# A convolution as products with diagonal matrices on the tensor engine, and the two batch elements of a quantiser taken one after the other

## The reference

```python
def bit_linear(x, w): return einsum('bsd,hd->bsh', act_quant(x), weight_quant(w))
def act_quant(x):                       # for each token
    scale = 127 / clip(max(abs(x), axis=-1), 1e-5)
    return clip(round(x * scale), -128, 127) / scale
# first block, hidden width 1024
h = bit_linear(x, w1)
h = depthwise_conv1d(h, conv_w, conv_b) # 3 taps along the tokens, padding 1
h = silu(h)
return bit_linear(h, w2)
# second block
return bit_linear(silu(bit_linear(x, w_gate)) * bit_linear(x, w_up), w_down)
```

## Time and profile before

| | us |
|---|---|
| median of 3 runs (lowest, highest) | 2870.0 (2860.18, 2885.66) |
| the profiled execution | 2874.32, span 2872.5 |
| busy: PE, DVE, ACT, POOL | 2015.8, 2128.5, 1306.5, 1243.8 |
| granted TensorE clock, mean share of full speed | 0.84 |

### The profile page before, as it was taken

One profiled execution on the slowest core, in us unless ns is written; L12 is line 12 of the kernel. 1 busy time (PEld: TensorE's weight loads), 2 busy tenths in 40 slices (PEclk: granted clock), 3 DMA queues, 4 the chain that ended last, 5 costly groups with the idle time before them and its releaser, 6 DMA issues.

```text
span 2872.5 us, 22420 instructions
## 1 busy us (share of the span) xinstructions
PE 2015.8 (70%) x7684; PEld 1072.3 (37%) x7684; DVE 2128.5 (74%) x2457; ACT 1306.5 (45%) x1838; POOL 1243.8 (43%) x535
## 2 busy tenths in 40 slices
PE   3786486677597847677668774777767966667775
PEld 1125362226322625223532253422452234542243
DVE  7753868995684495998768367799686827689967
ACT  1363445553155335654306443665421645356532
POOL 1030238991213024997211311599521221079942
PEclk9798588998789868899879976799977987689997
DMA  5500000000330000000061000000006100000000
GB/s 172 90 18 0 1 1 0 0 1 0 80 77 7 0 0 0 0 0 1 0 118 45 1 1 0 1 0 0 0 1 118 46 1 1 0 0 0 0 0 15
DMA packets 55914, 57.45 MB, mean 20 GB/s; under 512 B 8624, under 2 KB 50352, under 8 KB 55792
## 3 DMA queue, kind: packets, MB, share of 16 engines
q1 hardware_dynamic: 48880, 49.62, 6.8%
q10 hardware_dynamic: 6912, 6.29, 1.9%
HBM read 38.71 MB, written 16.79 MB: 19 GB/s over the span
## 4 chain that ended last, share of the span: by engine, by line
PE 44%; DVE 25%; POOL 14%; issue 7%; ACT 5%; DMA 3%; SPq 1%; ACTq 0%; POOLq 0%; DVEq 0%
PE psum L571 15%; PE psum L776 10%; POOL big L1507 9%; PE psum L671 4%; POOL big L1496 4%; DVE mid L1110 3%; PE psum L648 3%; PE psum L659 3%; PE psum L609 3%; DVE mid L1324 2%; PE psum L681 2%; ACT mid L833 2%; DVE big L1275 2%; DMA mid<-scratch 2%; DVE big L1149 2%
## 5 line engine op out<-in xcount | busy, mean ns | idle before, releaser
L776 PE MATMUL psum<-big,ident 128*128 128x512 f32 x992 | 524.0, 677 | 202.7 <-POOL big L1507 202.1
L1390 DVE TENSOR_TENSOR_SCAN big<-psum,b,big 128x512 f32<-128x512 f32 x512 | 613.9, 1259 | 0.0
L833 ACT ACTIVATE big<-psum 128x1024 f32<-128x1024 f32 (+2 forms) x592 | 451.9, 776 | 324.2 <-PE psum L659 252.1
L1507 POOL TENSOR_TENSOR big<-big 128x2048 f32<-128x2048 f32 x124 | 560.7, 4522 | 22.3 <-DVE big L1390 22.3
L833 ACT ACTIVATE psum<-mid,aneg 128x512 f32<-128x512 f32 x512 | 353.9, 692 | 265.0 <-DVE big L1390 265.0
L776 PEld LDWEIGHTS psum<-big,ident 128*128 128x128 f32 x992 | 202.1, 214 | 483.1 <-POOL big L1507 264.6
L1201 DVE TENSOR_REDUCE negmax<-psum 128x1 f32<-128x512 f32 x512 | 317.0, 678 | 68.1 <-PE psum L648 67.8
L648 PE MATMUL psum<-mid 96*128 96x512 bf16 x512 | 221.5, 438 | 65.6 <-DMA mid<-scratch 51.0
L1458 POOL TENSOR_TENSOR lsum<-lsum,onorm 128x512 f32<-128x512 f32 x32 | 40.6, 1270 | 523.7 <-ACT onorm L833 523.7
L1496 POOL TENSOR_TENSOR big<-mid,big 128x512 f32<-128x512 f32 (+1 forms) x128 | 222.9, 1742 | 20.0 <-ACT big L833 20.0
L1472 POOL TENSOR_TENSOR big<-big,mid 128x513 f32<-128x513 f32 x40 | 55.0, 1387 | 348.4 <-ACT big L833 348.4
(11 more groups left out here) (165 smaller groups left out, 3393.1 us busy)
## 6 DMA issues: line engine op xcount, KB each, us to landing
mid<-scratch SPq DMA_DIRECT2D x192, 64.0 KB, 2.2
scratch<-mid SPq DMA_DIRECT2D x4, 1536.0 KB, 6.0
mid<-scratch SPq DMA_DIRECT2D x48, 128.0 KB, 11.7
mid<-scratch ACTq DMA_DIRECT2D x48, 128.0 KB, 13.7
scratch<-big SPq DMA_DIRECT2D x4, 1536.0 KB, 25.8
out<-hres SPq DMA_DIRECT2D x8, 513.0 KB, 7.7
big<-in_x SPq DMA_DIRECT2D x8, 512.0 KB, 4.1
big<-in_w SPq DMA_DIRECT2D x2, 1024.0 KB, 6.3
```

Of the source, the lines that this page charges most:

```text
L776: mm = nc.tensor.matmul(y_psum[:, c], ident[:, :], st(1, k)[:, c], start=(n == 0), stop=(n == NS - 1))
L833: return nc.scalar.activation(o, a, func, **kw)
L1390: V.tensor_tensor_scan(st(0, k)[:, c], a_psum(DT * k + c), st(0, k)[:, c], b0[:, p, n, c:c + 1], ALU.mult, ALU.add).then_inc(scanned, 1)
L1507: G.tensor_tensor(st(1, k), st(0, k), c_row(k).unsqueeze(1).broadcast_to([P, DT, S]), ALU.mult).then_inc(hc_ready, 1)
```

## The change

In the first block, tiles 1, 2, 4 and 7 (`PE_CONV`) no longer get bias, middle tap and the two outer taps from ACT and DVE. PE computes all three taps: POOL prepares twelve 128 x 128 matrices, the identity with each row scaled by a tap (`tap(c, k)`, kept in `onorm`, which is free after attention), and PE multiplies the tile by them with the tile shifted by one column for each tap, in float32, into a PSUM slot of its own (`v{c}c`). ACT reads that slot, adds the bias and applies SiLU in one instruction. So that the shifted reads are defined at the edges, tiles of set 0 now lie 514 columns apart with a zero column ahead of each.

In both blocks the quantiser's second half is taken batch by batch: the transposes and rows of batch 0 come before those of batch 1 on PE, `scales(1, 0)` stands ahead of `absmax(1, 1)`, and DVE's multiplications and roundings alternate with `scales(1, 1)`. `absmax` of batch 0 stands one loop step earlier in both blocks.

```diff
+PE_CONV = (1, 2, 4, 7)
+CONV_LAG = 3
...
-    each(*[f"f{c}" for c in range(HT)])
+    for s in range(PAIR * HT + CONV_LAG):
+        if s < PAIR * HT:
+            order.append((f"f{s % HT}", s // HT))
+        if s >= CONV_LAG and (s - CONV_LAG) % HT in PE_CONV:
+            order.append((f"v{(s - CONV_LAG) % HT}c", (s - CONV_LAG) // HT))
...
         def big8(p, n):
-            o = p * 2 * W8 + n * W8
-            return big[:, o:o + W8].rearrange("p (c t) -> p c t", c=HT)
+            o = p * 2 * W8 + n * (W8 + 1)
+            if n:
+                return big[:, o:o + HT * T].rearrange("p (c t) -> p c t", c=HT)
+            return big[:, o:o + HT * (T + 1)].rearrange("p (c t) -> p c t", c=HT)[:, :, 1:T + 1]
...
+                def convolve(p, c):
+                    slot_free(f"v{c}c", p)
+                    o, f = slot(f"v{c}c", p), padded(p, c)
+                    for a, b in ((0, SPLIT), (SPLIT, T)):
+                        for k in range(3):
+                            mm = nc.tensor.matmul(o[:, a:b], tap(c, k), f[:, a + k:b + k], start=(k == 0), stop=(k == 2))
...
-                token_maxima(1)
-                token_rows(1)
+                for p in range(PAIR):
+                    token_maxima(1, (p,))
+                    token_rows(1, (p,))
...
-                    if 0 <= p < PAIR:
+                    if 0 <= p < PAIR and c not in PE_CONV:
                         act.wait_ge(f_pool if c in POOL_F else f_dve, tile_count(POOL_F, p, c))
...
+                    if 0 <= p < PAIR and c in PE_CONV:
+                        wait_full(act, f"v{c}c", p)
+                        run(big8(p, 1)[:, c], slot(f"v{c}c", p), ACT.Silu, bias=col("cb", c)).then_inc(f_silu, 1)
...
-                    if s == HT + 6:
+                    if s == HT + 5:
                         dve.wait_ge(f_silu, HT)
                         absmax(1, 0, big8(0, 1))
+                scales(1, 0)
                 dve.wait_ge(f_silu, HT * PAIR)
                 absmax(1, 1, big8(1, 1))
-                for p in range(PAIR):
-                    scales(1, p)
-                for p in range(PAIR):
-                    quantise(1, p, big8(p, 1), big8(p, 0), mid_bf(p, 5, HT), HT)
+                scale_tiles(1, 0)
+                scales(1, 1)
+                round_tiles(1, 0)
+                scale_tiles(1, 1)
+                round_tiles(1, 1)
...
-                    if s == HT + 4:
+                    if s == HT + 3:
                         dve.wait_ge(prod, HT)
                         absmax(3, 0, big8(0, 1))
+                scales(3, 0)
...
+                pool.wait_ge(unit_full, UNITS["O", PAIR - 1, 1] + 1)
+                for c in PE_CONV:
+                    for k in range(3):
+                        G.tensor_scalar(tap(c, k), ident[:, :], col("cw", 3 * c + k), 0.0, ALU.mult, ALU.add).then_inc(
+                            taps_ready, 1)
```

More of the change, by code:

```diff
@@ L94, in quantiser @@
     def quantiser(q):
-        each(f"T{q}")
-        each(f"I{q}", f"S{q}")
+        if q % 2:
+            each(f"T{q}", f"I{q}", f"S{q}")
+        else:
+            each(f"T{q}")
+            each(f"I{q}", f"S{q}")
     for p in range(PAIR):
@@ L112, in plan_fills @@
     each(*[f"z{c}" for c in range(DT)])
+    while len(order) % 4 != 2:
+        order.append(None)
     each("w0", "w1")
@@ L401, in build @@
         prod = signal("prod")
+        taps_ready = signal("taps_ready")
         raw_n = KT * HID
@@ L590, in layer_norm, with token_maxima @@
                         fill(f"var{q}", p, [(mean_w[:, :], sq[:, k]) for k in range(KT)])
-                def token_maxima(q):
-                    for p in range(PAIR):
+                def token_maxima(q, pairs=range(PAIR)):
+                    for p in pairs:
                         pe.wait_ge(absmax_part, q_of(q, p))
@@ L721, in _ @@
                 token_rows(0)
-                for p in range(PAIR):
-                    pe.wait_ge(q_ready, q_of(0, p))
-                    for c in range(HT):
-                        fill(f"f{c}", p, [(w1[:, k, c * P:(c + 1) * P], mid_bf(p, 1, 2)[:, k]) for k in range(KT)])
-                token_maxima(1)
-                token_rows(1)
+                for s in range(PAIR * HT + CONV_LAG):
+                    p, c = divmod(s, HT)
+                    if p < PAIR:
+                        if c == 0:
+                            pe.wait_ge(q_ready, q_of(0, p))
+                        fill(f"f{c}", p, [(w1[:, k, c * P:(c + 1) * P], mid_bf(p, 1, 2)[:, k]) for k in range(KT)])
+                    p, c = divmod(s - CONV_LAG, HT)
+                    if p >= 0 and c in PE_CONV:
+                        if s == CONV_LAG + PE_CONV[0]:
+                            pe.wait_ge(taps_ready, 3 * len(PE_CONV) + 2 * PAIR)
+                        pe.wait_ge(f_pool, tile_count(POOL_F, p, c))
+                        convolve(p, c)
+                for p in range(PAIR):
+                    token_maxima(1, (p,))
+                    token_rows(1, (p,))
                 for p in range(PAIR):
@@ L1467, in _ @@
                     G.memset(mid2(p, 3)[:, :, 0:1], 0.0).then_inc(pads, 1)
+                pool.wait_ge(unit_full, UNITS["O", PAIR - 1, 1] + 1)
[3 more added lines that the diff above has]
+                            taps_ready, 1)
+                for p in range(PAIR):
+                    for columns in pad_columns(p):
+                        G.memset(columns, 0.0).then_inc(taps_ready, 1)
                 for p in range(PAIR):
```

77 lines of the change are left out of this document (49 added, 28 removed).

## The result

| | before | after |
|---|---|---|
| median of 9 runs, us (lowest to highest) | 2871.2 (2860.18 to 2885.66) | 2851.8 (2838.79 to 2853.05) |
| the profiled execution, us | 2874.32 | 2838.79 |
| ratio after : before, 95% interval | | 0.992 (0.9899 to 0.9941) |

The change gains 0.8%.

A forecast was written before the change was run, and what follows sets the result against it. No engine was full; DVE alone was taken to bound the first block's tiles. (5.0 + 2.3 - 0.6) x 4 turns took 27 us off 2874.3, giving 2847; that execution lay 4.3 above the median, so 2843, range 2820 to 2866.

The forecast's parts named there:

- The taps: First block's tiles: tap work moved from DVE and ACT to PE brings X from 1050.0 to 1045.0, 5.0 us a turn.
- X: The end of the first block's second reduction over eight tiles, 1050.0 in the second turn before the change.
- C: Rival: PE at the low clock during the first block's convolutions, 12 us a turn slower, 2918 us; chance 0.12.
- The quantiser: First block from X to the last add: the new order takes 24.0 us against 26.3, 2.3 us gained a turn.
- The rounding: Quantiser's roundings on DVE: reading five runs and writing one takes 4.45 us a batch, the slow end, against 2.37.
- B: Rival: the rounding keeps its fast rate, 2.4 us for 4.45; 44 us off a run, 2826 us; chance 0.22.
- The second block: Second block: the second reduction begins later, behind slot reads and scales waiting for transposes; 0.6 us lost a turn.
- The sum: Whole run: 5.0 + 2.3 - 0.6 us a turn over 4 turns, 27 us off.
- D: Rival: hand-overs through PE, ACT and DVE eat the taps' gain, leaving 7 us a run, 2863 us; chance 0.21.

The follow-up runs named there:

- e6: The changed kernel with the first block's first reduction one step earlier in DVE's loop; ratio to before 0.9875.
- e11: The changed kernel with the quantisers' scaled tiles written without gaps, unscaled tiles still padded; 2829.1 us, ratio to before 0.9836.
- e3: The changed kernel with the rounded tiles also written with a gap between them and read so by PE; ratio to before 0.9873.
- e4: The kernel before with only the padded layout, set 0 in runs 514 columns apart; ratio to before 1.0053.
- e1: The kernel before with only the quantiser's new order, reductions at their old steps, table load moved; 2839.0 us, ratio to before 0.9886.
- e12: e11 and e6 together, with the second block's reduction of batch 0 back at its old step; 2819.4 us, ratio to before 0.9801.
- e8: The changed kernel with each convolution on PE cut to its middle product (wrong in value); one execution, 2842.4 us.
- e2: The changed kernel with both quantisers in the order of before and both reductions at their old steps; ratio to before 1.0007.

## Why the prediction was right, point by point

**The taps (5.0 us up to X).** Measured in the second turn: 3.9 (46.5 to 42.6). The bound moved to PE at the full clock, as said: granted clock 1.00 from 993 to 1025, and the last convolution ends at 1021.9, which settles C. A convolution took 2.76 where 2.6 was worked out from the float32 fills. The first reduction came at +22.4, predicted +22.0. The other two terms that were off are small: the second reduction started 12.9 behind the first, not 12.5, and took 7.29, not 7.0, with POOL's multiplication beneath it. The working named the left tap of tile 3 as what the first reduction stands behind, and DVE did wait 3.04 us there. It did not ask whether it has to stand there: e6 shows this place in the order to be worth 3 us a turn.

**The quantiser (2.3 us).** Measured 3.0: X to the end 23.3, predicted 24.0. Each station is within 0.3 us: batch 0 rounded at X + 8.7 (8.8), batch 1 at X + 17.6 (17.7). The working had POOL hold DVE's multiplication to X + 13.3; it took 4.43 and ended at X + 13.1. The end was 0.7 early because PE's second product ran at the full clock (1.00), 3.69 for the 4.4 that half of 8.83 gave.

**The rounding (4.45 a batch).** 4.49, with 2.83 for the five tiles. This was the open cost, and the end chosen was right; B is out for this kernel, and its price was near: 44 us a run was worked out for a fast rounding, and e11, which makes it fast, gains 48 by the blocks. Of the two reasons given one fails. The prediction took the slow end because the multiplication, too, has an operand that is not one run; but in e3 both operands of the rounding are in five runs, and it takes 2.90. What e3, e4 and e11 bear out is the comparison of source and destination: 2.37 for one run to one, 2.90 for five runs to five, 4.49 for five to one. The rule of the Trainium skill ("VectorE: DVE Perf Modes", section "What auto-detection actually checks") names outermost counts that are both even or equal; the trace agrees in all three cases.

**The second block (-0.6 us).** Measured -0.76 in the mean, -0.85 in the second turn, but by another split. Predicted was a second reduction 3.6 us late, because of the moved step with its slot reads, and the wait of `scales(3, 0)` for the transposes. It came 2.5 late, and e1 has nearly the same (+29.8) with the step unmoved: so the wait and the `scales` themselves are the cause. The step is worth 0.7 a turn (e12 against e11). The rest, from the last rounding to the last add, took 7.2 us for the 6.3 predicted, with PE's product at 5.26 and a granted clock of 0.69 in it, where 4.4 was reckoned.

**The sum.** 27 us predicted, 26.6 by the blocks, 35.5 between the two profiled executions, 19.4 between medians. That 27 and 26.6 agree is partly luck: in the second turn the taps gave 1.1 less than predicted and the quantiser 0.7 more, 24.3 us in four turns, and the rest comes from before's first and fourth turns, whose first blocks ended 1 us later. D (hand-overs eat the gain) is out as a whole, since the first reduction did move, but e8 shows where it begins: 3.4 us below the present pace.

**What the prediction did not see** is the sign of the parts. It gave 5.0 of 6.7 us to the products. Taken alone they and their layout give 1.1 us a turn (e2), and the order alone 7.5 (e1), because there it keeps the fast rounding: the slow one costs 5.4 us a turn with the new order (e11) and only 2.3 with the old (e4). The surplus of 5.75 and 5.13 in the earlier trace rows was named and priced, but inside the change, where slow rounding gives half of it back. Pricing each part against before on its own, from the same rows, would have shown a part that does better alone.

## What to carry to other kernels

Where a new layout serves one reader (here the shifted reads of a convolution), give the later consumers the old one: the rewrite in between costs nothing and saved 21.5 us by the blocks. Price each part of a combined change alone, since a part can be worth more without the others. After moving work to an idle engine, look at the place of the reductions and waits in the relieved engine's hand-written order (a step of one tile was worth 3 us a turn), and count tiles from both sides: by the blocks four tiles on PE were better than two and than five, though in whole runs only five was told apart.

## What the runs showed of the hardware

- The same rounding of eight tiles from float32 to bf16 takes 2.37, 2.90 or 4.49 us by the gaps alone: one run to one, five runs to five, five to one.
- DVE and POOL exclude each other in some pairs, and the later one waits. DVE's multiplication and POOL's, started together, take 2.83 and 5.73, or 3.08 and 5.75, nearly the sum of both for the later one. The fast rounding beside POOL is held: its five tiles take 1.50 us alone and 4.26 where POOL's multiplication is running (before, e1, e11). The slow rounding is not: 2.83 beside POOL (e4) and without it, and POOL's 3.09 beside it in after is not held either. The Trainium skill ("GPSIMD Engine Reference", section "Specifications") tells of contention with DVE instructions in a 2-port mode or with two SBUF inputs; the trace agrees for the multiplication (two inputs) and for both forms of the rounding (only the fast one waits for POOL).
- The reduction over eight tiles, which has one source, takes 7.05 us with POOL idle (second reduction of before) and 7.24 to 7.32 with 3.1 us of POOL's multiplication beneath it, 3 to 4% more; that section has no word on such an instruction. The first block's first reduction takes 7.45 in after and 7.26 in e8, with 1.1 us of POOL beneath it in both, so something besides POOL adds to it there.
- PE's clock after a pause. The last 32 matmuls take 3.69 us at a granted clock of 1.00 and about 5 us or more where it has fallen, and no single number seen here decides which. They took 3.69 after 1.84 us of pause (e1), 4.97 after 3.41 (e3) and 5.26 after 4.15 (after). But a pause of 3.35 in the first block of after was followed by 3.69. Two turns with the same pause went either way:

```profile
2118.85 5.79 PE L603 MATMUL psum<-mid,wd 128*128 128x257 bf16 x32
2127.47 3.69 PE L603 MATMUL psum<-mid,wd 128*128 128x257 bf16 x32 [2.83 <-DVE mid L1097]
...
352.70 3.69 PE L574 MATMUL psum<-mid,w 128*128 128x257 bf16 x32
359.26 5.25 PE L574 MATMUL psum<-mid,w 128*128 128x257 bf16 x32 [2.86 <-DVE mid L1048]
```

The first pair is after, second block, third turn; the second is e1, first block, first turn. There the faster first product was the one with a slow product behind it, as in e8 (4.15, then 6.60). A faster product also lengthens the pause behind it by ending early: in e3 against e1 (3.70 for 4.43) by 0.7 of the 1.6 us more of pause. Which of the two acts was not tried.
